# Squares of 32x32 on VectorE: who transposes the gated activation of chunks 0 and 1

## What is computed

```python
def lora_add(base, inp, A, B):
    Ab = A[layer_idx][lora_indices]
    Bb = B[layer_idx][lora_indices]
    t = jnp.einsum('bri,bni->bnr', Ab, inp)
    return base + jnp.einsum('bor,bnr->bno', Bb, t) * SCALE
gate = lora_add(jnp.einsum('bnh,fh->bnf', x, W_gate), x, A_gate, B_gate)
up = lora_add(jnp.einsum('bnh,fh->bnf', x, W_up), x, A_up, B_up)
act = jax.nn.silu(gate) * up
down = lora_add(jnp.einsum('bnf,hf->bnh', act, W_down), act, A_down, B_down)
...
x = x + _L1_cond_ref(x, ...)
```

## Time and profile before

| | |
|---|---|
| Time, median of 3 runs | 559.76 us (559.27 to 559.87) |
| The profiled execution: time, span from first to last instruction | 559.44 us, 557.6 us |
| Mean granted TensorE clock over the span | 0.995 |
| Busy in the span: PE, PEld (weight loads), DVE, ACT, POOL | 93%, 85%, 47%, 36%, 7% |
| The 16 tiles | from 80.9 us to the end, one every 29.42 us in the loop |
| Busy DMA engines in the loop | about a fifth |

### The profile page before, as it was taken

One profiled execution on the slowest core, in us unless ns is written; L12 is line 12 of the kernel. 1 busy time (PEld: TensorE's weight loads), 2 busy tenths in 40 slices (PEclk: granted clock), 3 DMA queues, 4 the chain that ended last, 5 costly groups with the idle time before them and its releaser, 6 DMA issues.

```text
span 557.6 us, 10117 instructions
## 1 busy us (share of the span) xinstructions
PE 519.3 (93%) x3169; PEld 472.5 (85%) x3169; DVE 260.4 (47%) x558; ACT 199.9 (36%) x427; POOL 39.8 (7%) x55
## 2 busy tenths in 40 slices
PE   0098899999999999999999999999999999999997
PEld 0097787989898989999898989898989898999986
DVE  7894266544444435353435353534444443435341
ACT  4890008333333433243323233323333343324221
POOL 1015700100000000000000000000000000000000
PEclk9999899999999999999999999999999999999999
DMA  7799991312030404030303031211203040403000
GB/s 288 293 303 389 325 322 44 78 47 78 22 105 6 118 0 117 6 111 13 111 13 106 18 92 32 83 41 52 71 22 101 7 116 0 120 3 111 13 21 19
DMA packets 32306, 53.19 MB, mean 95 GB/s; under 512 B 7586, under 2 KB 16194, under 8 KB 32290
## 3 DMA queue, kind: packets, MB, share of 16 engines
q1 hardware_dynamic: 32290, 53.00, 31.0%
HBM read 48.69 MB, written 4.28 MB: 95 GB/s over the span
## 4 chain that ended last, share of the span: by engine, by line
PE 86%; DVE 6%; DMA 4%; ACT 1%; issue 1%; SPq 0%; DVEq 0%
PE ps_g L962 21%; PE ps_u L962 20%; PE ps_db L1000 13%; PE ps_da L1000 13%; PE ps_x L991 3%; PE ps_x L942 3%; PE ps_g L916 2%; DMA toep<-kpad 2%; PE ps_u L916 2%; PE ps_g L972 2%; PE ps_u L972 2%; PE ps_g L973 2%; PE ps_u L973 2%; DMA kpad<-k_sb 2%; PE ps_x L1034 1%
## 5 line engine op out<-in xcount | busy, mean ns | idle before, releaser
L470 ACT CAST b_spl<-b_raw 64x512 fp32r<-64x512 f32 (+1 forms) x96 | 54.4, 569 | 98.6 <-PE ps_u L973 79.5
L780 DVE TENSOR_TENSOR b_spl<-b_raw,b_spl 64x512 fp32r<-64x512 f32 (+1 forms) x96 | 60.4, 630 | 53.7 <-ACT b_spl L470 50.1
L962 PE MATMUL ps_g<-w_hi,x_hi 128*128 128x512 f32 (+1 forms) x192 | 72.7, 379 | 1.4 <-DVE x_lo L874 1.4
L962 PE MATMUL ps_u<-w_hi,x_hi 128*128 128x512 f32 (+1 forms) x192 | 71.4, 372 | 0.0
L962 PE MATMUL ps_u<-w_lo,x_hi 128*128 128x512 f32 (+1 forms) x192 | 71.3, 371 | 0.0
L962 PE MATMUL ps_u<-w_hi,x_lo 128*128 128x512 f32 (+1 forms) x192 | 71.3, 371 | 0.0
L962 PE MATMUL ps_g<-w_lo,x_hi 128*128 128x512 f32 (+1 forms) x192 | 71.1, 370 | 0.0
L962 PE MATMUL ps_g<-w_hi,x_lo 128*128 128x512 f32 (+1 forms) x192 | 71.0, 370 | 0.0
L816 DVE TENSOR_TENSOR h_act<-h_act,ps_u 128x512 f32<-128x512 f32 (+1 forms) x48 | 30.3, 632 | 54.3 <-PE ps_u L973 54.2
L1000 PE MATMUL ps_da<-wd_hi,ht_hi 128*128 128x288 f32 (+1 forms) x176 | 54.6, 310 | 0.0
L1000 PE MATMUL ps_db<-wd_hi,ht_hi 128*128 128x288 f32 (+1 forms) x176 | 53.3, 303 | 0.0
(11 more groups left out here) (169 smaller groups left out, 894.4 us busy)
## 6 DMA issues: line engine op xcount, KB each, us to landing
a_raw<-atab SPq DMA_DIRECT2D x64, 152.0 KB, 2.4
toep<-kpad SPq DMA_DIRECT2D x16, 512.0 KB, 6.8
b_raw<-btab SPq DMA_DIRECT2D x128, 64.0 KB, 2.1
um<-xr SPq DMA_DIRECT2D x16, 256.0 KB, 4.7
x<-xT SPq DMA_DIRECT2D x8, 512.0 KB, 7.9
w_raw<-wgu SPq DMA_DIRECT2D x8, 512.0 KB, 9.1
out<-y_sb SPq DMA_DIRECT2D x15, 256.0 KB, 2.1
b_raw<-btab SPq DMA_DIRECT2D x64, 44.0 KB, 1.8
```

Source lines behind the costliest of these rows:

```text
L470: nc.scalar.copy(b_spl[0:LR, up, 0:w], b_raw[slot][:, up * w:(up + 1) * w]).then_inc(b_hi, 1)
L780: V.tensor_tensor(b_spl[LR:P, up, 0:w], b_raw[slot][:, up * w:(up + 1) * w], b_spl[0:LR, up, 0:w].bitcast(F32), ALU.subtract).then_inc(b_l ...
L962: T.matmul(ps[:, 0:w], xs[:, q, kb, :], ws[:, kb, col:col + w], start=(kb == 0 and xs is x_hi and ws is w_hi), stop=False)
```

## The change

VectorE takes over the transposes of chunks 0 and 1. It transposes squares of 32x32: one instruction reads 32 tokens (32 partitions) and the 32 columns at the same place in each of the four blocks of 128, so four squares, 128 elements in each partition, and writes them into `ps_x`. A chunk takes 16 such instructions, 4 of token groups by 4 of column groups, written in two halves of 8 with other work of VectorE between them. The target partitions go round 0, 32, 64, 96 with each instruction. Chunk 2 (352 columns, the last block not full) is still transposed by TensorE. Two things are put in another order: on ScalarE the high part of chunk 1's transposed activation comes before the next tile's two `b_hi` copies, and on VectorE the next tile's second `b_lo` goes behind `x_lo`.

```diff
--- before.py
+++ after.py
@@ -24,6 +24,7 @@
 NM = 64
 NF = 1376
 FB = -(-NF // P)
+Q = 32
 FLAST = NF - (FB - 1) * P
 R = 16
 BT = 4
@@ -531,10 +532,10 @@
                     top_part(NP_GU + 5)
                 ht_hi_part(0)
                 silu(2)
+                ht_hi_part(1)
                 if not last:
                     b_hi_part(na, nq, 0, 0)
                     b_hi_part(na, nq, 0, 1)
-                ht_hi_part(1)
                 act.wait_ge(res_ps, t + 1)
                 wait(act, y_out, 16 * t)
                 nc.scalar.copy(y_sb[:, :], ps_x[0][:, :]).then_inc(res_ok, 1)
@@ -815,6 +816,28 @@
                     dve.wait_ge(u_ps, n + 1)
                     V.tensor_tensor(h_act[:, s, 0:w], h_act[:, s, 0:w], ps_u[s][:, 0:w], ALU.mult).then_inc(act_ok, 1)
 
+                def transpose_act(c, froms):
+
+                    nf, w = BLK[c][1], CH[c][1]
+                    s = (NC * q + c) % 2
+                    bank = [0, 1, 1][c]
+                    if froms[0] == 0:
+                        dve.wait_ge(act_ok, NC * t + c + 1)
+                        if c == 0:
+                            dve.wait_ge(tm_ok, t + 1)
+                        elif c == 1:
+                            wait(dve, tdlo_ok, t)
+                        else:
+                            dve.wait_ge(htlo_ok, (NC + 1) * t + 2)
+                    for tok in froms:
+                        for to in range(P // Q):
+                            n = len(range(to * Q, w, P))
+                            flat = h_act[tok * Q:(tok + 1) * Q, s, :].rearrange("t (f q) -> t f q", q=P)
+                            into = ps_x[bank][to * Q:(to + 1) * Q, :].rearrange("q (f t) -> q f t", t=P)
+                            ins = V.transpose(into[:, 0:n, tok * Q:(tok + 1) * Q], flat[:, 0:n, to * Q:(to + 1) * Q])
+                    if froms[-1] == P // Q - 1:
+                        ins.then_inc(ht_ps, 1)
+
                 def ht_lo_part(c):
                     f0, nf = BLK[c]
                     bank = [0, 1, 1][c]
@@ -837,6 +860,7 @@
                 b_lo_part(a, q, 1, 0)
                 gated(0)
                 b_lo_part(a, q, 1, 1)
+                transpose_act(0, (0, 1))
                 if not first:
                     finish(t - 1)
                 dve.wait_ge(bd_hi, t + 1)
@@ -845,21 +869,23 @@
                 if first:
                     rem_part(NP_GU + 2)
                     rem_part(NP_GU + 3)
+                transpose_act(0, (2, 3))
                 b_lo_part(a, q, 2, 0)
                 gated(1)
                 b_lo_part(a, q, 2, 1)
+                transpose_act(1, (0, 1))
                 if first:
                     rem_part(NP_GU + 4)
                     rem_part(NP_GU + 5)
                 ht_lo_part(0)
+                transpose_act(1, (2, 3))
+                gated(2)
                 if not last:
                     b_lo_part(na, nq, 0, 0)
-                gated(2)
-                if not last:
-                    b_lo_part(na, nq, 0, 1)
                 ht_lo_part(1)
                 if not last:
                     x_lo_part(na, nq, False)
+                    b_lo_part(na, nq, 0, 1)
                 ht_lo_part(2)
                 dve.wait_ge(ad_ps, t + 1)
                 wait(dve, td_ps, t)
@@ -973,22 +999,14 @@
                     T.matmul(ps[:, 0:w], t_lo[:, up, :], b_spl[:, up, 0:w], start=False,
                              stop=True).then_inc(u_ps if up else g_ps, 1)
 
-                def transpose_act(c):
-                    f0, nf = BLK[c]
-                    s = (NC * q + c) % 2
-                    bank = [0, 1, 1][c]
-                    pe.wait_ge(act_ok, NC * t + c + 1)
-                    if c == 0:
-                        pe.wait_ge(tm_ok, t + 1)
-                    elif c == 1:
-                        wait(pe, tdlo_ok, t)
-                        if first:
-                            pe.wait_ge(amaskt_ok, 1)
-                    else:
-                        pe.wait_ge(htlo_ok, (NC + 1) * t + 2)
+                def transpose_last():
+                    f0, nf = BLK[NC - 1]
+                    s = (NC * q + NC - 1) % 2
+                    pe.wait_ge(act_ok, NC * t + NC)
+                    pe.wait_ge(htlo_ok, (NC + 1) * t + 2)
                     for f in range(nf):
                         rows = P if f0 + f < FB - 1 else FLAST
-                        ins = T.transpose(ps_x[bank][0:rows, f * P:(f + 1) * P], h_act[:, s, f * P:f * P + rows],
+                        ins = T.transpose(ps_x[1][0:rows, f * P:(f + 1) * P], h_act[:, s, f * P:f * P + rows],
                                           ident[:, :])
                     ins.then_inc(ht_ps, 1)
 
@@ -1023,11 +1041,9 @@
                 for up in range(2):
                     base(1, up)
                     lora(1, up)
-                transpose_act(0)
                 for up in range(2):
                     base(2, up)
                     lora(2, up)
-                transpose_act(1)
 
                 pe.wait_ge(htlo_ok, (NC + 1) * t + 1)
                 for kb in range(KB):
@@ -1038,7 +1054,7 @@
                     pe.wait_ge(w_rem_dve, len(pieces) - NP_POOL)
                 pe.wait_ge(ad_lo, t + 1)
                 down_chunk(0)
-                transpose_act(2)
+                transpose_last()
                 pe.wait_ge(htlo_ok, (NC + 1) * t + 2)
                 down_chunk(1)
                 if not last:
```

## The result

The changed kernel takes **615.75 us** (615.32 to 616.03, four runs) against 559.76 before: 1.0998 of the time, interval 1.0979 to 1.1018. The forecast was 605.3, so the direction is right and the size is 10.4 us short. The profiled execution spans 613.5 us, 55.9 more than before.

What follows compares the result with a forecast made beforehand. TensorE was taken as the bound, busy all 29.42 us of a tile. Loop 35.8, first tile 8.4 and last 1.3 together add 45.6 us, taking the profiled 559.44 to 605.0, median 605.3; range 585 to 650.

Steps and rivals of the forecast that it cites:

- the two predicted places: TensorE, each loop tile: residual transposes wait 1.97 us for `ht_lo(0)`, chunk 2's transposes 1.47 us for `ht_lo(1)`.
- The `b_hi` step: ScalarE: next tile's `b_hi` copy, behind `ht_hi(1)`, ready at 342.00; VectorE's `b_lo` waits for it, ahead of `ht_lo(1)`.
- Doubt about `b_lo(2,0)` in the loop: VectorE: `b_lo(2,0)` ends at 333.79, just when TensorE wants it; any delay is swallowed by the following wait.
- so 0.32: VectorE: transposes start 0.32 us apart, as the four `t_lo` do, because the target partitions change at every instruction.
- the forecast's own rate: VectorE's chain: all 32 transposes of a tile lie in it, so each 0.01 us of distance is worth 5.1 us.
- 14 tiles of the loop: Loop: chunk 2's transposes start at 343.50 instead of 340.94, so each tile is 2.56 us longer, 35.8 in all.
- first tile: First tile: low parts of the down weights share VectorE's chain; chunk 2's transposes start at 114.0, not 105.58: 8.4 us.
- last tile: Last tile: no next tile, so `ht_lo(1)` follows `ht_hi(1)` and TensorE loses 1.3 us.
- The lower clock: Rival: TensorE falls to 1.2 GHz after waits, hidden after a tile's first; 628 us. Chance 0.16, shared with dearer transposes.
- The fall after the second wait: TensorE, after its wait for `ht_lo(1)`: a clock fall there costs 1.54 us, 15 times, giving 628 us.
- The faster rival: VectorE between two transposes: they overlap at 0.21 us distance, TensorE never waits in the loop, 551.5 us. Chance 0.13.
- break-even distance of 0.231: VectorE: the change wins if transposes start less than 0.231 us apart, from 0.32 - 45.6 / 512.

Runs made afterwards that it cites:

- e9_c0: Changed kernel with chunk 0 alone transposed on VectorE, chunk 1 back on TensorE, orders as changed: 564.14 us, 1.0093 of the kernel before.
- e3_half: Changed kernel with each transpose taking two squares instead of four, same number of instructions: 580.55 us, 1.0381 of the kernel before.
- e6_htfirst: Changed kernel with `ht_lo(1)` ahead of the next tile's `b_lo` on VectorE: 601.26 us, 1.0729 of the kernel before.
- e1_same: Changed kernel with each transpose writing into the partition group that it reads: 560.85 us, 1.0037 of the kernel before.
- e2_swap: Changed kernel with the two transpose loops swapped, so the group read changes at every instruction: 615.64 us, 1.1013 of the kernel before.

## Why the forecast was right, and where it was short

**The mechanism held, step by step.** TensorE loses its place as the bound, VectorE's row from `gated(0)` to `ht_lo(1)` sets the tile, and the loss shows at the two predicted places. Predicted waits 1.97 and 1.47, measured 1.82 and 1.45; counted from start to start, as the forecast counts them, 1.98 and 1.66 (367.16 and 372.77 are where the rows before them would have let TensorE start). That the first fits so well is luck: at the measured distance it should have been 2.38, 24 transposes at 0.017 more. But `b_lo(2,0)` makes TensorE 0.35 late ahead of it. The `b_hi` step (0.47 to the second copy, then `b_lo` 0.63 after it starts) measured 0.49 and 0.65 (`ht_hi(1)` on ScalarE starts at 371.83, the copies at 372.32, `b_lo` at 372.97). Doubt about `b_lo(2,0)` in the loop was settled as forecast: it is late, but its delay lies inside the wait that follows. These are TensorE's rows in the changed kernel, where the middle one starts 0.41 after the first and the last 0.26 after the middle one, against 0.16 in the row:

```profile
364.06 0.32 PE L988 MATMUL ps_g<-w_hi,x_lo 128*128 128x352 f32 x1
364.47 0.43 PE L998 MATMUL ps_g<-b_spl,t_hi 128*128 128x352 f32 x1
364.73 0.32 PE L999 MATMUL ps_g<-b_spl,t_lo 128*128 128x352 f32 x1
```

In e9_c0, without that wait, the same delay costs 0.36.

**What was mis-sized: the distance between transposes.** Taken 0.32 from the `t_lo`, measured 0.337. The step that failed is the reading "so 0.32", since `t_lo` runs 0.29 and a gap, and a transpose of as many elements runs 0.323 and a gap. By the forecast's own rate of 5.1 us for each 0.01 that is 8.7 of the missing 10.4 us. The rate itself was right: e3_half gives 35.2 us for 0.068 (5.2 per 0.01). The rest of the miss is small terms that the forecast had at nothing, and by luck an earlier start takes off nearly what the lower clock of the last tile adds.

The sum, term by term, in us of the profiled spans (tiles measured from one `t_m` to the next):

| Term | forecast | measured | of the difference |
|---|---|---|---|
| 14 tiles of the loop | 14 x 2.56 = 35.8 | 14 x 3.21 = 44.9 | 0.55 per tile from the distance, 0.10 from small gaps |
| first tile | 8.4 | 9.0 | the distance |
| last tile | 1.3 | 3.1 | 0.55 the distance, the rest a lower clock |
| before the tiles | 0 | -1.1 | the start is that much earlier in this execution; over the profiled executions of all kernels here the first `t_m` starts between 83.1 and 85.5 |
| all | 45.6 | 55.9 | |

**The lower clock** was a rival at 628 us, with the remark that a fall after the first wait "hides in the second". That is what happened. The next two rows are windows of 5 us right after the first wait in two tiles of the changed kernel, and the transposes that end the stretch:

```profile
140.00:145.00 5.00, 4.27 (x21) 4.27 (x22) 4.23 (x11) 1.58 (x4) 1.17 (x2) 0.66 0.05 14
173.00:178.00 5.00, 3.84 (x28) 3.60 (x28) 4.20 (x12) 1.96 (x4) 1.17 (x2) 1.00 0.01 2
```

```profile
140.73 0.66 PE L1050 MATMUL ps_x<-ident,xt 128*128 128x128 f32 x4 [1.82 <-DVE ht_lo L846]
146.02 0.55 PE L1009 MATMUL ps_x<-ident,h_act 128*128 128x128 f32 x3
173.35 0.66 PE L1050 MATMUL ps_x<-ident,xt 128*128 128x128 f32 x4 [1.81 <-DVE ht_lo L846]
178.64 0.55 PE L1009 MATMUL ps_x<-ident,h_act 128*128 128x128 f32 x3 [1.45 <-DVE ht_lo L846]
```

In the first of the two the mean granted clock is 0.66, and the second wait is gone from the row; yet both stretches last 5.29 us from row to row. TensorE ran slower inside time that it would have waited out. Four of the fourteen loop tiles are so, where the forecast had said a clock of 1.00. The fall after the second wait, which would have cost 1.54 each time, was not seen in the loop: from tile to tile it is 32.62 to 32.64 throughout. Where there is no second wait, the fall costs: in e6_htfirst, and in the last tile, whose stretch takes 5.20 instead of 3.63:

```profile
597.56 0.66 PE L1050 MATMUL ps_x<-ident,xt 128*128 128x128 f32 x4 [1.82 <-DVE ht_lo L846]
602.76 0.49 PE L1009 MATMUL ps_x<-ident,h_act 128*128 128x128 f32 x3
```

**The faster rival** (transposes that overlap, 551.5) fell in the changed kernel, for the reason given against it. Its break-even distance of 0.231 could be tried: in e1_same the mean distance is 0.230 (1.82, 1.87 and 1.82 for three eights), and the kernel takes 1.0037 of the time before. At 0.230 the forecast's sum gives 0.5 less than the kernel before, and e1_same takes 1.4 more; at 0.337 it gives 54.3 more, and the changed kernel takes 56.0. So the equation behind the forecast holds to within 2 us from 0.23 to 0.34.

## What to carry to other kernels

Work moved from a full engine to a half-idle one is free only as long as it fits into the idle time ahead of each step that the full engine waits for: here sixteen transposes per tile fit (1.2% faster, once `b_lo(2,0)` went ahead of eight of them and the first tile was left to TensorE; 0.9% slower without these two) and thirty-two cost 10%. Where many small instructions are moved, their distance matters more than their duration, so look in the trace for two neighbours of the same partition pattern, and take as their price the duration of the operation itself and the gap, not that of an arithmetic one of the same size. Where an engine has become the bound, put ahead in its row what the others wait for: `ht_lo(1)` before the next tile's `b_lo` gave back a quarter of the loss.

## What was not expected of the hardware

- A held transpose of 32x128 fp32 into PSUM is recorded at 0.323 us, an unheld one at 0.27, so being held lengthens the distance from 0.20 to 0.33 and the recorded duration too. The masked products of the same element count were 0.21 apart.
- A change of the group that is read holds the next instruction as a change of the group that is written does (e2_swap).
- Waits of 1.8 us were followed by some 3.5 us at 1.2 GHz in some tiles (four of the loop's fourteen, in the changed kernel and in e6_htfirst) and by none in others, with rows that are otherwise alike. What decides between them stays open.
